# A fused attention and mixture-of-experts kernel: the order of the two expert layers, the place of one PSUM wait, and the steps of some side pieces are changed

## What is computed

```python
xn = layernorm(x)                                   # B=4, S=1024, D=128
# attention, 16 heads of 8
Q = rope(xn @ Wq.T); K = rope(xn @ Wk.T); V = xn @ Wv.T
attn = softmax(Q @ K.T / sqrt(8)); a = (attn @ V) @ Wo.T
# mixture of experts, 8 experts, the 2 best of each token
w, idx = top_k(xn @ Wg, 2); w = softmax(w)
h = relu((xhat * gamma[e] + beta[e]) @ W1[e] + b1[e])    # 128 -> 512
y = sum over the two experts of w * (h @ W2[e] + b2[e] + xn)
out = x + a + y
```

## Time and profile before

| | us |
|---|---|
| median of 3 runs (lowest, highest) | 579.19 (578.89, 579.42) |
| the profiled execution | 579.44 |
| span of its trace | 577.6 |
| PE busy | 537.2 (93%) |
| ACT busy | 500.6 (87%) |
| DVE busy | 295.2 (51%) |
| POOL busy | 245.2 (42%) |

### The profile page before, as it was taken

How to read it: one execution, slowest core, us unless ns; L and a number is a source line. 1 busy time by engine, 2 the same in 40 slices (tenths; PEclk the granted TensorE clock), 3 DMA queues, 4 the chain that set the end, 5 groups by cost and what they waited for, 6 DMA issues and landing times.

```text
span 577.6 us, 12513 instructions
## 1 busy us (share of the span) xinstructions
PE 537.2 (93%) x4620; PEld 244.5 (42%) x4620; DVE 295.2 (51%) x986; ACT 500.6 (87%) x552; POOL 245.2 (42%) x308
## 2 busy tenths in 40 slices
PE   8899988899899999999899999999989999999875
PEld 6323322234445555335344555433434554555212
DVE  4975698854334444544443344455333444344394
ACT  2699998899998888998888988889889889888993
POOL 4289910798244444456222344365412443432100
PEclk9999999999999999999999999999999999999998
DMA  7045311533244454233533355531434454562451
GB/s 261 25 120 146 117 48 27 188 101 119 75 123 167 147 193 156 84 101 129 160 124 106 112 190 170 168 101 52 145 95 138 152 167 128 174 190 73 163 226 61
DMA packets 44656, 75.47 MB, mean 131 GB/s; under 512 B 7584, under 2 KB 17872, under 8 KB 44080
## 3 DMA queue, kind: packets, MB, share of 16 engines
q1 hardware_dynamic: 39232, 63.71, 34.2%
q0 software_dynamic: 4544, 9.32, 5.3%
q10 hardware_dynamic: 816, 1.61, 0.7%
HBM read 33.88 MB, written 8.85 MB: 74 GB/s over the span
## 4 chain that ended last, share of the span: by engine, by line
PE 74%; ACT 11%; DVE 8%; issue 3%; DMA 2%; ACTq 1%; POOL 0%; POOLq 0%; DVEq 0%; SPq 0%
PE acc L732 32%; PE sc L697 12%; ACT ring L963 11%; PE aside_bank L776 10%; PE sc L793 10%; PE sc L765 3%; PE aside_bank L802 2%; DVE x L1352 1%; PE aside_bank L608 1%; DMA wr<-L_attn_W_k 1%; DMA xn<-token_out 1%; PE aside_bank L793 1%; PE aside_bank L592 1%; DVE blocks L1131 1%; DMA token_out<-work,token 1%
## 5 line engine op out<-in xcount | busy, mean ns | idle before, releaser
L963 ACT ACTIVATE ring<-sc 128x1024 f32<-128x1024 f32 x512 | 487.6, 1031 | 53.8 <-PE sc L697 53.1
L732 PE MATMUL acc<-ring,v 128*9 128x512 f32 x2048 | 249.2, 594 | 14.1 <-ACT ring L963 9.3
L544 POOL DMA_INDIRECT work<-normed,token x71 | 69.6, 981 | 201.5 <-DVE work L1322 176.2
L697 PE MATMUL sc<-qs,ks 32*128 32x512 f16 x1024 | 101.4, 384 | 8.8 <-ACT ring L963 6.5
L697 PEld LDWEIGHTS sc<-qs,ks 32*128 32x128 f16 x1024 | 26.3, 90 | 165.0 <-ACT ring L963 145.7
L732 PEld LDWEIGHTS acc<-ring,v 128*9 128x9 f32 x2048 | 40.7, 89 | 114.2 <-issue 80.5
L556 POOL DMA_INDIRECT token_out<-work,token x71 | 70.4, 992 | 38.9 <-issue 19.2
L1328 DVE TENSOR_SCALAR work<-aside_bank,xn 128x128 f32<-128x128 f32 x216 | 60.8, 344 | 24.2 <-PE aside_bank L776 24.2
L1339 DVE TENSOR_TENSOR work<-sc,xn 128x128 f32<-128x128 f32 x50 | 14.6, 292 | 108.6 <-PE sc L793 108.6
L776 PE MATMUL aside_bank<-work,xn 128*128 128x128 f32 x432 | 57.6, 276 | 0.0
L776 PEld LDWEIGHTS aside_bank<-work,xn 128*128 128x128 f32 x432 | 52.6, 192 | 1.1 <-issue 1.1
(11 more groups left out here) (202 smaller groups left out, 440.9 us busy)
## 6 DMA issues: line engine op xcount, KB each, us to landing
xn<-w_rest SPq DMA_DIRECT2D x54, 323.0 KB, 3.3
xn<-L_ffn_W SPq DMA_DIRECT2D x54, 256.0 KB, 2.8
w_last<-w_rest SPq DMA_DIRECT2D x17, 323.0 KB
w_last<-L_ffn_W SPq DMA_DIRECT2D x17, 256.0 KB
qs<-hl SPq DMA_DIRECT2D x60, 64.0 KB
ks<-hl SPq DMA_DIRECT2D x60, 64.0 KB
x<-L_attn_x SPq DMA_DIRECT2D x4, 512.0 KB, 8.7
w_rest<-L_ffn_W SPq DMA_DIRECT2D x8, 256.0 KB, 3.9
```

The lines of the kernel that those rows point to most:

```text
L544: pool.indirect_dma_start(out=xt[t % TILE_BUFFERS], out_offset=None, in_=xh_d[:, :], in_offset=bass.IndirectOffsetOnAxis(ap=token[:, 0, t: ...
L697: last = nc.tensor.matmul(dst, ks[r:r + 32, kb * P:(kb + 1) * P], qs[r:r + 32, at], start=True, stop=not slow)
L732: last = nc.tensor.matmul(acc[32 * j:32 * j + VW, :], v9[:, b, kb, 4 * g + j, :], ring[:, (2 * n + j // 2) % UNITS, j % 2, :], start=(kb = ...
L963: nc.scalar.activation(ring[:, (2 * n + u) % UNITS, :, :], sc[HOME[2 * n + u]][:, :].rearrange("p (h c) -> p h c", h=2), ACT.Exp, scale=SC ...
```

## The change

It has five parts. (1) In 23 pairs of `BOTH`, those whose preceding pair is not in `BOTH` (`ONE_FIRST`), PE does layer one before layer two and the transpose. (2) After such a pair n, scores(n+2) avoid the spare buffer; both of its groups go to the two buffers of scores(n+1), and PE waits for DVE's reading one body later, ahead of scores(n+3). (3) `tiles_are_taken` is gone; PE waits for DVE's reading only in the pair behind a layer-two-only pair. (4) There are four split tiles instead of five, at chosen pairs (layer two alone at 78, 90, 142, 206 and, for the last tile, 238). (5) Batch 1's projections move from 38, 40, 46, 50 to 38, 44, 48, 50, its norms from 56 to 58, and the squares to odd steps behind a pair of `BOTH`; `SPLIT_ROUND` follows.

```diff
-PLAIN_AT = {n: (1, r) for r, n in enumerate((38, 40, 46, 50))}
+PLAIN_AT = {n: (1, r) for r, n in enumerate((38, 44, 48, 50))}
...
-NORM_AT = {PER_BATCH * b - 8: b for b in range(1, B)}
+NORM_AT = {PER_BATCH * b - (6 if b == 1 else 8): b for b in range(1, B)}
...
-SECOND_PAIRS = []
-for m in range(MORE):
-    SECOND_PAIRS.append(next(n for n, k in zip(FREE[1:], FREE) if n >= PER_BATCH + (STEPS - PER_BATCH) // MORE * m
-                             and n not in SECOND_PAIRS and k not in SECOND_PAIRS and n not in SIDE and k not in SIDE))
+SECOND_PAIRS = [PER_BATCH * b + n for n in (14, 26) for b in range(1, B)][:MORE]
...
+ONE_FIRST = [n for n in BOTH if n - 2 not in BOTH]
...
-SQUARE_AT = {n + 5: piece for n, piece in PLAIN_AT.items() if piece[0] > 1}
-SQUARE_AT.update({n: (1, r) for r, n in enumerate((43, 45, 50, 54))})
-SPLIT_ROUND = {piece: 3 if n < FFN_FROM else 5 + max(k for k, step in TWO_STEP.items() if step < n)
+SQUARE_AT = {next(m for m in (n + 7, n + 5, n + 9) if m - 1 in BOTH): piece for n, piece in PLAIN_AT.items() if piece[0] > 1}
+SQUARE_AT.update({n: (1, r) for r, n in enumerate((47, 53, 55, 57))})
+SPLIT_ROUND = {piece: 4 if n < FFN_FROM else 5 + max([k for k, step in TWO_STEP.items() if step < n], default=0)
                for n, piece in SINE_AT.items()}
...
+        before = n - 2 if n - 2 in ONE_FIRST else None
         for u in range(2):
-            pair = order[0]
+            pair = next(k for k in order if before is None or k != spare[before])
...
-            def tiles_are_taken(n):
-                wait(pe, tile_taken, len([m for m in TWO_AT if m < n]))
...
             def aside(n):
-                tiles_are_taken(n)
+                if n - 2 in TWO_AT and n - 2 not in BOTH:
+                    pe.wait_ge(tile_taken, TWO_AT[n - 2] + 1)
...
+                if n in ONE_FIRST:
+                    layer_one(ONE_AT[n])
                 if n in TWO_AT:
                     layer_two_and_turn(TWO_AT[n], n)
-                if n in ONE_AT:
+                if n in ONE_AT and n not in ONE_FIRST:
                     layer_one(ONE_AT[n])
...
                         pe.wait_ge(e_ok, NEED[2 * n + 3])
-                        if n - 1 in BOTH:
-                            pe.wait_ge(tile_taken, TWO_AT[n - 1] + 1)
+                        for pair in (n - 1, n - 2):
+                            if pair in BOTH and (pair in ONE_FIRST) == (pair == n - 2):
+                                pe.wait_ge(tile_taken, TWO_AT[pair] + 1)
```

## The result

The changed kernel takes 571.36 us (median of 3 runs, 570.46 to 572.47) against 579.19: a ratio of 0.9866, interval 0.9838 to 0.9895. The forecast was 570.0, in a range of 567.6 to 575.3. The profiled execution took 571.36 us with a span of 569.5, against 579.44 and 577.6.

What follows compares the result with a forecast made beforehand. PE bounds pairs with both layers behind another such pair (4.53 us), ACT layer-one-only and light pairs (3.67). Terms gave -7.5 us for pairs 42 to 238 and -1.95 for 38 and 40: -9.4, so 570.0 us, range 567.6 to 575.3.

Steps and rivals of the forecast that it cites:

- The new order: Layer one first in 23 pairs behind light pairs: 4.58 us instead of 4.81, stall shrinking from 0.28 to 0.05.
- the two terms of the sum: Spare-buffer stall gone in 17 pairs, 17 x 0.28 = 4.76 us; score-buffer wait added in 23, 23 x 0.05 = 1.15.
- Pair 42: First pair of the stretch, no layer two yet: +0.73 us over 3.85, since scores(44) wait to +2.42.
- The wait for the reading: Weighing behind five layer-two-only pairs no longer waits for DVE: 4.09 to 3.67 us each, 2.10 us gone.
- The squares: Squares leave light pairs for odd steps where ACT waits for PE anyway: 3.3 us gone, 0.06 to spare.
- Batch 1's rotations: Pair 40 loses its projection and falls from 5.69 to 3.74 us: -1.95; pair 38 keeps its time.
- A: Rival: new order gains nothing, 23 pairs stay at 4.81, +5.3 us, so 575; 12%.
- C: Rival: wait behind layer-two-only pairs only moves, or squares do not fit, +1.5 to +3 us, 572.5; 10%.
- E: Rival: all gains small enough to cancel with the dearer pair 42 and the split, no change; 3%.
- D: Rival: slower, restart after ACT's exponentials costs each of 23 pairs; decides at pairs of 5.04 us; 581; 5%.
- B: Rival: POOL holds DVE's division at step 48 for 1.64 us, stalls worth 1 to 2 us, 571.5; 10%.
- My two signs by the clock: Scores of step 43 at about 108.0 us instead of 109.9, scores of step 241 at about 531.

Runs made afterwards that it cites:

- e9: Changed kernel with pair 42 out of ONE_FIRST and the wait for the second exponential only before the second group of scores(n+2); 570.77 us, ratio 0.9843.
- e1: Changed kernel with ONE_FIRST empty, so layer two and the transpose come first in every pair; ratio 0.9900 to the kernel before.
- e5: Kernel before with only batch 1's projections, norms and squares moved, split rounds with them; ratio 0.9955 to the kernel before.
- e7: Changed kernel with the wait for DVE's reading at the head of every side work again, odd bodies too; ratio 1.0024 to the kernel before.
- e4: Changed kernel with the squares of batches 2 and 3 back at n + 5; ratio 0.9874 to the kernel before.
- e3: Changed kernel with PE waiting for DVE's reading in the odd body again behind layer-two-only pairs; ratio 0.9941 to the kernel before.
- e6: Changed kernel, layer one first kept, but scores(n+2) on the spare buffer again, DVE's reading awaited before them; ratio 1.0159 to the kernel before.
- e11_changed_again: Changed kernel unedited, run again on the same chip as the kernel before's repeat; ratio 0.9857 to the kernel before.
- e10: Kernel before, unedited, run again for its profile; one run, 584.05 us.
- e0: Changed kernel unedited, run again; 577.65 us beside 583.16 for the kernel before, ratio 0.9921.

## Why the prediction was right, and where its sizes were off

**The new order.** Right in place, and in size for the pair: 4.58 forecast and measured. The reason that I gave for the 0.05 was at most half of it. I had PE ready at +2.34 and waiting for ACT to +2.42. ACT's second exponential and PE's own side work both end for +2.42, and e9 shows that PE's is enough: my 2.02 us for the side work came from the old order, and the new one takes 2.09. That the two meet at the same time is luck. What the order is worth by itself is 3.65 us (e1). It looks like the two terms of the sum, 4.76 less 1.15, but isn't the same thing: those count 17 pairs of the old tables, and e1 has 22 at other places, with pair 42 against them.

**Pair 42.** Sized at 4.58, it took 4.85, 0.27 us more, and over the 4.7 that I had named as the sign of being wrong; the other 22 stayed under it. The cause was wrong too. I charged the whole rise over 3.85 to the new order, but in the old order and the same tables it takes 4.66 (e1), and with batch 1's pieces moved alone 4.49 (e5). Only 0.19 us are the order's. The rest comes with part 5: pair 40 is shortened, and pair 42 comes before ACT and the weights are ready for it. In the new order ACT has the exponential that scores(44) need only at +2.63 (100.66 + 11.30 = 111.96), not at +2.37.

```profile
100.66 11.30 ACT L964 ACTIVATE ring<-sc 128x1024 f32<-128x1024 f32 x12
...
109.33 0.39 PE L694 MATMUL sc<-qs,ks 32*128 32x512 f16 x4
...
111.66 0.41 DVE L1323 TENSOR_SCALAR work<-sc,xn 128x128 f32<-128x128 f32 x1 [2.72 <-DMA xn<-w_rest]
...
112.02 0.40 PE L694 MATMUL sc<-qs,ks 32*128 32x512 f16 x4 [1.10 <-ACT ring L964]
...
114.18 0.39 PE L694 MATMUL sc<-qs,ks 32*128 32x512 f16 x4
```

The third row shows a second lateness behind the first: DVE's reading waits for the tile's weights. It costs nothing here, but it is what scores(44) wait for in e1 (0.41), e5 (0.24) and e9 (0.52), once they don't wait for ACT.

**A term that the sum lacked.** Pairs n with n + 2 a multiple of 16, where the next quad of heads begins, take 0.09 or 0.10 more if PE waits for ACT there; 94, 158 and 222, where PE is the bound, keep 4.53. After, that is 46, 62, 126, 190 (4.67 or 4.68), 78, 142, 206, 238 and 110, 174 (3.76); before it was 46, 62 and 238 alone. Seven more pairs, +0.67 us. Against them stand the pairs at 128 and 192, the first of a batch, which took 4.64 before and 4.53 after: -0.22. With pair 42 this makes 0.72 of the 0.88 us that pairs 42 to 238 stand above the sum (6.62 gained, 7.5 forecast). The 0.16 left are small terms, among them pair 48, which carried 0.19 of the stall before where I counted 0.28. In the four at 4.67 and 4.68 it goes when the wait is split (e9). At a new quad one more wait, for the stack, stands ahead of the same matmul; at 128 and 192 there is one more ahead of the side work, for the new batch's values. That points to the number of waits in front of one instruction, but no run tries it by itself, so the cause isn't shown.

**The wait for the reading.** Right as a mechanism: DVE's reading no longer holds PE anywhere. Its price in the new order, 10.75 us (e7), was nowhere in the prediction, which counted only the 2.1 us of the old one. The five waits of the old tables held 2.10; after, pairs 78, 142 and 206 take 3.76 and not 3.67 (238 did so before as well), so 1.83 came from them, the difference being the term above.

**The squares.** Right: 2.88 us for the eight of batches 2 and 3 (e4), none with an effect on the exponential behind it, no pair at 5.14, and 3.85 nowhere. The 0.06 to spare was real.

**Batch 1's rotations.** Pair 40 took 3.72 (3.74 forecast), and 38 and 40 together gave 1.97 (1.95 forecast).

**Rivals.** A, that the new order gains nothing, fell with the pairs at 4.58. C fell with e3, e4 and the readings, E with the interval. D needed pairs of 5.04; the wait for the reading alone brings them to 5.02 (e7), and e6 beyond, so the case is close by, and the change avoids it with the wait one body later. Of B the collision happened, and its price didn't. At step 48 of the changed kernel POOL's sum and DVE's division meet:

```profile
122.84 1.25 POOL L530 TENSOR_TENSOR turned<-turned,rotated 128x512 f32<-128x512 f32 x1
...
123.71 0.55 DVE L1139 TENSOR_TENSOR att<-blocks,rec 128x128 f32<-128x128 f32 x1
```

The division ends 0.17 us behind POOL's sum (124.26 and 124.09) and takes 0.26 more than its 0.29. Before, it ended at 107.17, 0.16 behind a sum that ended at 107.01. In e11_changed_again, the same program, the sum ends at 123.51, and the division, started at 123.33, takes 0.33. So what such a meeting costs is what is left of POOL's instruction, and this one began near its end. That agrees with the Trainium skill, "SBUF — State Buffer", section "Who interferes with whom"; what I mis-sized is to price it at the full 1.64. No wait of PE followed from it. The row of 1.93 us isn't wholly explained, though: that division started at 105.24, 0.49 us ahead of the sum (105.73), and what held it until then isn't shown.

**Start and tail.** I wrote that nothing behind 240 changes. The tail was 0.9 shorter and the start 1.44 longer, and neither belongs to the change: e10, the kernel before, starts its scores at 26.91, and e0, the changed kernel, has a tail of 37.69. My two signs by the clock, scores(43) at about 108.0 and scores(241) at about 531, came at 109.33 and 533.17; less the 1.44 of the start that is 107.89 and 531.73. The warm-up's second block of 24 matmuls, of which the changed kernel's row follows, took 2.84 us before and 3.86 in e10. It started at 6.91 and 10.21 there, as soon as the first weights were in.

```profile
7.20 4.38 PE L572 MATMUL sc<-ones 128*128 128x128 f32 x24
```

24 matmuls in 2.84 us start 0.11 us apart, at a granted clock of 1.00, the level of 2.4 GHz. After, they start 0.21 us apart up to 10.4 and 0.11 behind it. The view gives 1.00 for 7.20 to 10.40 as well, but the trace's first record of the clock stands at 10.41, so that 1.00 is no reading. In e10 there is a record: the same spacing of 0.21 at 0.50, the level of 1.2 GHz.

```profile
10.00:12.20 2.20, 2.20 (x12) 2.20 (x12) 0.00 (x0) 1.65 (x11) 2.01 (x6) 0.50 0.97 385
```

The last output projection (eight matmuls, behind a wait of 2.20 us for DVE in both) took 2.08 us before and 1.16 after, which is the tail's whole difference; e0 has the 2.08 too. The windows of those stretches, the granted clock behind the five busy times, first before (half of full speed, 1.2 GHz), then after (full, 2.4 GHz):

```profile
572.30:574.50 2.20, 2.08 (x8) 1.78 (x8) 0.04 (x1) 0.00 (x0) 0.00 (x0) 0.50 0.03 7
```

```profile
565.20:566.40 1.20, 1.16 (x8) 0.97 (x8) 0.00 (x0) 0.00 (x0) 0.00 (x0) 1.00 0.05 14
```

**What stays open.** Why e0's comparison has 0.06 to 0.74 us more at 26 pairs of the changed kernel isn't known. The kernel before was slower there too, by less (583.16 against 579.19), but has no trace of it. The chip alone isn't the reason, since e1, e4, e5 and e6 ran on it without late pairs. e0's rows show exponentials that start 0.6 to 0.8 us behind their scores instead of 0.43, here in e0_same_again:

```profile
181.28 0.40 PE L694 MATMUL sc<-qs,ks 32*128 32x512 f16 x4
...
182.08 8.46 ACT L964 ACTIVATE ring<-sc 128x1024 f32<-128x1024 f32 x9 [0.60 <-PE sc L694]
```

It isn't in e11, so the ratio is 0.9857 and 0.9866 in two comparisons and 0.9921 in this one.

## What to carry to other kernels

Before you swap two blocks of work on an engine, list which buffer each block holds when the next consumer asks, and for how long its reader still needs it: here the swap alone costs 14.6 us beside the old order, and with the score buffers re-dealt and the reader's wait moved one body later it gains 3.65. Price a stall by what is left of the work in front of it, and look at which pairs an added wait falls on: ten pairs here take 0.1 us more where one more wait stands ahead of a matmul, though nothing that it waits for is late (that the wait is the cause isn't shown). When a pair gets dearer, undo the parts of the change one by one before you name the part: pair 42's rise was nearly all another part's. And read a change by stages between fixed instructions, which repeated to 0.01 us in two comparisons, rather than by the median, which moves with the start by some 1.5 us; but look at single pairs too, since in a third comparison the stage itself took 7.5 us more.

## What was not expected of the hardware

The same side work (a transpose and two layers) takes 2.05 us with layer two first and 2.09 with layer one first. The start of the kernel varies by 4.5 us between profiles (scores(0) at 22.56 to 27.05) with the arrival of the first weights and the rate of the warm-up's matmuls, while the stretch of the experts repeats to 0.01 us in e10 and e11. And one comparison adds up to 0.74 us at fixed pairs of a program that shows none of it in two others, though the chip of that comparison runs the next one without it.
